# Loads in order of need with a semaphore for each group, the first image in two halves, keys and queries handed over head by head

## The reference

```
xn = group_norm(x)                       # per image
q  = q_w @ xn + q_b                      # 1x1 convolution, 256 -> 256
xd = conv2x2_stride2(xn, ds_w) + ds_b    # 1024 -> 256 pixels
xd = layernorm_over_channels(xd) * ln_w + ln_b
k, v = kv_w @ xd + kv_b                  # two 256 -> 256 products
o  = softmax(q k^T / sqrt(32)) v         # 8 heads of 32 channels
x  = x + proj_w @ o + proj_b
```

## Time and profile before

| | us |
|---|---|
| runs | 898.1, 899.11, 899.64 |
| median | 899.11 |
| profiled execution | 893.1 |
| its span, first to last instruction | 891.3 |
| PE busy | 668.2 (75%) |
| DVE busy | 627.6 (70%) |
| ACT busy | 389.7 (44%) |
| mean granted clock | 0.843 |

### The profile page before, as it was taken

How to read it: one execution, slowest core, us unless ns; L and a number is a source line. 1 busy time by engine, 2 the same in 40 slices (tenths; PEclk the granted TensorE clock), 3 DMA queues, 4 the chain that set the end, 5 groups by cost and what they waited for, 6 DMA issues and landing times.

```text
span 891.3 us, 9082 instructions
## 1 busy us (share of the span) xinstructions
PE 668.2 (75%) x3272; PEld 306.1 (34%) x3272; DVE 627.6 (70%) x1117; ACT 389.7 (44%) x623; POOL 32.8 (4%) x26
## 2 busy tenths in 40 slices
PE   2967984997898999999888879886876766387100
PEld 2622532433232354443334442232343222255100
DVE  2555416614958752776788779987889969986897
ACT  0202451558647467556636267715526453101100
POOL 3200000200001000000020000002000000000000
PEclk9965998899998989899989789998895687685655
DMA  8040024000150000004000000020000100001001
GB/s 303 15 122 2 1 68 116 1 1 1 49 135 2 3 0 1 1 1 118 19 1 1 1 1 1 18 78 1 1 1 0 47 1 1 0 0 48 0 0 47
DMA packets 14990, 26.85 MB, mean 30 GB/s; under 512 B 3250, under 2 KB 6994, under 8 KB 14819
## 3 DMA queue, kind: packets, MB, share of 16 engines
q1 hardware_dynamic: 11648, 22.80, 8.6%
q10 hardware_dynamic: 3298, 3.48, 1.3%
HBM read 14.09 MB, written 4.19 MB: 21 GB/s over the span
## 4 chain that ended last, share of the span: by engine, by line
PE 54%; DVE 24%; ACT 13%; issue 4%; SPq 2%; DMA 2%; DVEq 0%; ACTq 0%
PE aD L1517 5%; PE bA L1409 5%; PE aA L1536 4%; DVE NEGMAX L955 4%; PE bA L1550 4%; PE pp L1442 3%; PE aA L1502 3%; PE bA L1638 3%; PE aD L1482 3%; PE aD L1536 3%; ACT PT L503 2%; PE pp L1409 2%; DVE ACC L1280 2%; DVE PA_ L1271 2%; DVE HB L1266 2%
## 5 line engine op out<-in xcount | busy, mean ns | idle before, releaser
L955 DVE TENSOR_REDUCE NEGMAX<-aD 128x2 f32<-128x512 f32 x128 | 82.8, 685 | 34.2 <-PE aD L1482 32.6
L503 ACT ACTIVATE PT<-aA 128x512 f32<-128x512 f32 x128 | 70.2, 594 | 83.4 <-PE aA L1502 82.7
L1482 PE MATMUL aD<-KST,QST 96*128 96x256 f16 x256 | 54.2, 322 | 28.4 <-DVE NEGMAX L955 16.5
L1280 DVE SCALAR_TENSOR_TENSOR ACC<-PA_,COEF,ACC 128x1024 f32<-128x1024 f32 x48 | 61.5, 1282 | 1.2
L1502 PE MATMUL aA<-QST,KST 98*128 98x512 f16 x128 | 47.7, 426 | 13.7 <-ACT PT L503 9.4
L1271 DVE TENSOR_TENSOR PA_<-HB 128x1024 f32<-128x1024 f32 x40 | 49.0, 1225 | 1.0
L1266 DVE TENSOR_TENSOR HB<-PA_ 128x1024 f32<-128x1024 f32 x40 | 48.7, 1217 | 0.1
L1482 PEld LDWEIGHTS aD<-KST,QST 96*128 96x128 f16 x256 | 20.5, 105 | 78.4 <-DVE NEGMAX L955 40.7
L1517 PE MATMUL aD<-PT,VT 128*32 128x512 f32 x256 | 37.8, 665 | 5.0 <-DVE NEGMAX L955 2.0
L790 POOL TENSOR_TENSOR GA<-GA,PT 128x1024 f32<-128x1024 f32 x8 | 19.3, 2428 | 575.0 <-ACT PT L531 575.0
L972 DVE TENSOR_TENSOR GA<-GA,aD 128x512 f32<-128x512 f32 x16 | 10.9, 684 | 41.5 <-ACT GA L516 33.7
(11 more groups left out here) (298 smaller groups left out, 1325.4 us busy)
## 6 DMA issues: line engine op xcount, KB each, us to landing
XF<-in_x SPq DMA_DIRECT2D x4, 1024.0 KB, 5.1
QST<-QH SPq DMA_DIRECT2D x32, 128.0 KB, 2.4
XR<-in_x SPq DMA_DIRECT2D x4, 1024.0 KB, 5.0
out<-ACC SPq DMA_DIRECT2D x4, 1024.0 KB, 4.0
QST<-QL SPq DMA_DIRECT2D x16, 128.0 KB, 2.5
PS<-in_cw ACTq DMA_DIRECT2D x1, 1152.0 KB
WDS<-in_wds SPq DMA_DIRECT2D x1, 1024.0 KB, 8.2
WP<-in_wp SPq DMA_DIRECT2D x2, 256.0 KB, 10.9
```

Source lines behind the costliest of these rows:

```text
L503: e.activation(PROB[:, 4 * kt + j, :], SLOT[f"aA{j % 2}"][:, :], ACT.Exp)\
L955: e.tensor_reduce(NEGMAX[:, h, 2 * j:2 * j + 2], SLOT[f"aD{j % 2}"][:, :].rearrange("p (t k) -> p t k", t=2), AX.X, ALU.max, negate=True). ...
L1280: e.scalar_tensor_tensor(out=acc, in0=interior(PA_, cc), scalar=COEF[:, cc, k:k + 1], in1=acc, op0=ALU.mult, op1=ALU.add).then_inc(*dve_m. ...
L1482: mm = e.matmul(s[:, t * NK:(t + 1) * NK], QST[0:96, h, qt * P:(qt + 1) * P], KST[0:96, h, :], start=True, stop=True)
```

## The change

The loads on SP keep their order but for WP1 and WP0, which change places, and get four semaphores: `down_loaded` (COL, WDS), `query_loaded` (WQ), `kv_loaded` (WK, WV) and `mid_loaded` (WP1, WP0, XPR, DTP). Each engine waits for those that it uses. x comes as two DMAs, one for each channel half, with a semaphore each, for every image. ACT's 14 loads are issued in its `setup`, behind the group norm's two steps. What needs the middle group (the fold of WP1, WD, the projections) moves behind the keys, into `setup_projections` on PE and DVE.

The front's order becomes: downsampling, queries of block row 0, statistics of the keys' layer norm, queries of block row 1 (second half first), keys, values. The copies on SP are ordered by head at their end, with one semaphore for each `j`; head h < 4 of the scores waits for the five copies of `j` = h and for ACT's one. The order strings of all engines are new. In `SP_ORDER`, the residual load of an image now always stands ahead of the next image's stacking (before, image 2's stood between the queries and the keys of image 3).

```diff
-gn0 ds q0_0 q0_1 q1_0 q1_1 msq0 k vT
+gn0 ds q0_0 q0_1 msq0 q1_1 q1_0 k vT
...
-F5 A3 F5 A3 F5 A2 F2 A1 F2 A2 M1 A1 M3
+F4 A3 F4 A3 F4 A3 F3 A2 M1 A1 M3
...
-            sp.dma_start(XF[:, :, :], x_v[:, 0:CC, :]).then_inc(x_loaded, 16)
+            for cc in range(CC):
+                sp.dma_start(XF[:, cc, :], x_v[:, cc, :]).then_inc(x_loaded[cc], 16)
             sp.dma_start(MAT[:, :, :], mats).then_inc(mats_loaded, 16)
-            for dst, src in ((COL, cols), (WDS, wds), (WQ, wq), (WK, wk), (WV, wv), (WP0, wp0),
-                             (WP1, wp1), (XPR, xpr), (DTP, dtp)):
-                sp.dma_start(dst[tuple(slice(None) for _ in dst.shape)], src).then_inc(early_loaded, 16)
+            for loaded, pairs in ((down_loaded, ((COL, cols), (WDS, wds))), (query_loaded, ((WQ, wq),)),
+                                  (kv_loaded, ((WK, wk), (WV, wv))), (mid_loaded, ((WP1, wp1), (WP0, wp0), (XPR, xpr), (DTP, dtp)))):
+                for dst, src in pairs:
+                    sp.dma_start(dst[tuple(slice(None) for _ in dst.shape)], src).then_inc(loaded, 16)
...
+                def copy(dst, quad, j, src):
+                    sp.dma_start(dst[32 * quad:32 * quad + 32, j:HEADS:4, :], src[32 * j:32 * j + 32, :, :]).then_inc(stacked[j], 16)
+
                 sp.wait_ge(*pe_a.at(b - 1, "st3_1_3"))
...
+                sp.wait_ge(*act_f.at(b, "qh1_0"))
+                for j in range(4):
+                    for quad in (0, 2):
+                        copy(QST, quad, j, QH)
+                yield
+                sp.wait_ge(*dve_f.at(b, "ql1_0"))
+                for j in range(4):
+                    copy(QST, 1, j, QL)
+                yield
+                sp.wait_ge(*act_f.at(b, "kh1"))
+                copy(KST, 0, 0, KH)
+                copy(KST, 0, 1, KH)
+                sp.wait_ge(*dve_f.at(b, "kl1"))
+                copy(KST, 2, 0, KL)
+                copy(KST, 2, 1, KL)
+                for j in (2, 3):
+                    copy(KST, 0, j, KH)
+                    copy(KST, 2, j, KL)
+                yield
...
-                e.wait_ge(early_loaded, 16 * EARLY_N)
+                e.wait_ge(down_loaded, 32)
+                e.wait_ge(kv_loaded, 32)
                 columns("bA0", 0, WK, "kv_ln_b")
-                columns("bA0", 2, WV, "kv_ln_b")
-                columns("bA0", 4, WP1, "ln_b").then_inc(*pe_set.step("fold"))
+                columns("bA0", 2, WV, "kv_ln_b").then_inc(*pe_set.step("fold"))
+
+            def setup_projections():
+
+                e.wait_ge(mid_loaded, 64)
...
-                if h == 0:
-                    e.wait_ge(stacked, 16 * STACK_DMAS * b + 16 * STACK_DMAS)
-                    e.wait_ge(second_stacked, 16 * SECOND_DMAS * b + 16 * SECOND_DMAS)
+                if h < 4:
+                    e.wait_ge(stacked[h], 16 * STACK_DMAS * b + 16 * STACK_DMAS)
+                    e.wait_ge(second_stacked[h], 16 * b + 16)
...
-            def query(b):
-                for m, half in BLOCKS:
+            def query(b, m):
+                for half in (m, 1 - m):
```

More of the change, by code:

```diff
@@ L121 @@
 PE_SETUP = """
-fold wd fold0 wpc
+fold fold1 wd fold0 wpc
 """
@@ L401, in load @@
             def load(b):
-                sp.wait_ge(*pe_f.at(b - 1, "q1_1"))
-                sp.dma_start(XF[:, :, :], x_v[:, b * CC:b * CC + CC, :]).then_inc(x_loaded, 16)
+                sp.wait_ge(*pe_f.at(b - 1, "q1_0"))
+                for cc in range(CC):
+                    sp.dma_start(XF[:, cc, :], x_v[:, b * CC + cc, :]).then_inc(x_loaded[cc], 16)
                 yield
@@ L432, in _ @@
         def _(e):
-            for dst, src in ((S16, small16), (W1S, w1s), (IPX, ipx), (IPZ, ipz), (XB, xb), (XC, xc), (OPW, opw),
-                             (W2Q, w2q), (W2K, w2k), (W2V, w2v), (WP2, wp2), (ROWS, rows), (KIDX, kidx)):
-                e.dma_start(dst[tuple(slice(None) for _ in dst.shape)], src).then_inc(late_loaded, 16)
-            e.dma_start(CW, cw.partition_broadcast(P)).then_inc(late_loaded, 16)
             for s in (act_f, act_a, act_c, act_b, act_d, act_m):
@@ L695, in stream_f @@
                 yield from down(b)
-                yield from query(b)
+                yield from query(b, 0)
                 yield from rstd(b, 0, VAR0, act_f, dve_f)
+                yield from query(b, 1)
                 yield from keys(b)
@@ L741, in setup @@
             def setup():
-                e.wait_ge(early_loaded, 16 * EARLY_N)
+                for dst, src in ((S16, small16), (W1S, w1s), (IPX, ipx), (IPZ, ipz), (XB, xb), (XC, xc), (OPW, opw),
+                                 (W2Q, w2q), (W2K, w2k), (W2V, w2v), (WP2, wp2), (ROWS, rows), (KIDX, kidx)):
+                    e.dma_start(dst[tuple(slice(None) for _ in dst.shape)], src).then_inc(late_loaded, 16)
+                e.dma_start(CW, cw.partition_broadcast(P)).then_inc(late_loaded, 16)
+                e.wait_ge(down_loaded, 32)
                 e.activation(NEGA[:, :], COL[:, :, COLS.index("A_log")], ACT.Exp).then_inc(*act_set.step("expA"))
@@ L835, in group_norm @@
                     for half in range(2):
+                        if l == 0 and half == 0:
+                            e.wait_ge(x_loaded[cc], 16 * b + 16)
                         e.bn_stats(STAT[:, cc, half, :], src(cc, half)).then_inc(*dve.step(f"gn_st{l}_{cc}{half}"))
@@ L1724, in stream_f @@
                     setup()
+                    yield
                 yield from down(b)
-                yield from query(b)
+                yield from query(b, 0)
                 yield from kv_norm(b)
+                yield from query(b, 1)
+                yield from keys(b)
                 if b == 0:
                     setup_projections()
-                yield from keys(b)
+                    yield
             def stream_a(b):
```

128 lines of the change are left out of this document (66 added, 62 removed).

## The result

The changed kernel takes 911.94 us (median of 4 runs, 910.08 to 913.92), the kernel before 899.38 us in the same comparison (4 runs, 898.1 to 901.43): ratio 1.0138, 95% interval 1.0109 to 1.0167. It is **slower** by 1.4%, where the prediction said 889 us. Timed once more beside the last experiments it came to 911.99 us with a ratio of 1.0197 (1.0147 to 1.0246).

A forecast was written before the change was run, and what follows sets the result against it. No single engine bounds it: four images share one interleaved pipeline whose front is paid in full. Part 1 -7.2, Part 2 -2.7, Part 3 0: -9.9 us from 899.11 gives 889 us, range 880 to 898 (own range 886 to 891).

The forecast's parts named there:

- Part 1: Image 0's front: a semaphore per load group lets PE's setup start earlier; downsampling ends at 26.2, not 33.39: -7.2 us.
- the prediction's formula: Downsampling time as 6.97 us plus 0.218 us for each instruction at half clock level; 18.6 such instructions forecast.
- What left the front: ACT's 14 load issues, folding WP1 and WP0, WD and the centring, moved later: hidden behind other work, costing nothing.
- Part 2: Image 0, downsampling to first score: statistics between queries and copies by head, head 0 needing only copies 1 to 15: -2.7 us.
- Part 3: Images 1 to 3 and the new order: up to -4.2 at block 1's group norm against up to +4.5; taken as 0.
- The last sentence of the sum: Behind 57 us: a shift of the front reaches the end whole unless an order holds it back; 889 us.
- Rival C: Image 2's scores start late: up to +13.4 us of products and sums ahead of them, 903 us; chance 0.10.
- A: Image 0's front: the clock rises no earlier, or WV lands late; head gives 7.0 to 7.8, 892 us; chance 0.15.
- B: Images 1 to 3: the new order gives its 4.2 us on top and more at later images, 885 us; chance 0.18.
- D: From 750 us on, DVE must finish image 2's maxima, so the front's gain is used up: 899 us; chance 0.07.
- The residual load ahead of image 3's copies: On SP, image 2's residual load could hold image 3's copies; 7 us of slack, so part of C's chance only.

The follow-up runs named there:

- the old order with the same means: Changed kernel with the order strings of before and statistics again behind both query rows, all else of the change kept: 883.52 us, ratio 0.9844.
- the inner order in image 0: All of the change under the old order strings, plus, in image 0 alone, statistics between the two query rows: 886.22 us, ratio 0.9899 to the kernel before.
- the cut at image 1's front: Changed kernel with its order until image 1's front is through (about 130 us), the old order from there: median 890.99 us, ratio 0.9826 to the kernel before.

## Why the prediction was wrong

- **Part 1 was right in its mechanism**, and gave 1.0 us more than forecast. Fold at 11.58 (forecast 11.72), no DMA in front of it, downsampling at 15.1 (15.16). It took 10.08 us, which by the prediction's formula is 14 instructions at half level (18.6 forecast): the rise came near 21.4, 7.7 us earlier than before and not 5.7. So it ended at 25.2, 8.2 us earlier than before, where 7.2 were forecast. What left the front stayed hidden; the centring of W2V (28.44 to 30.75) is in the chain, as it was before.
- **Part 2 gave 0.5 us and not 2.7.** SP's first copy came at the downsampling's end + 10.8 (9.75 forecast), since the second split query stands behind the centring; the fourteen issues ahead of the last needed copy took 10.2 us and not 9.0. No head after the first waits for its copies, as forecast.
- **Part 3 is the failed step**: "I take 0, between ends of nearly equal size", with +4.5 as the upper end. By the ratios (1.0138 and 1.0197 against 0.9844) the new order costs 3.0 to 3.6%, 26 to 32 us; at like clock 22 us (912.00 against 889.79). The working behind that zero looked at one place, from 140 to 174 us, and there it was fair: against the old order with the same means, image 0's convolution starts 2.0 us earlier (161.88 against 163.84) and PE is 2.2 us behind by 280 us. The three places above where PE then idles lie behind it, and none was in the bounds. That the order was dealt anew on four engines was treated as one trade of a hole against a job, though its strings differ from image 1 to the last.
- **The last sentence of the sum** ("a shift of the front reaches the end whole unless an order holds it back") is borne out in its first half only roughly: with the old order 8.0 us at the head were 14.6 at the end in an execution at 0.851, and 9.9 were 5.4 at 0.837 with the inner order in image 0. The exception decided.
- **Rival C** named the place and part of the size: image 2's first score at 272.15, 6.6 us later than before (forecast 3.5), the total slower. Its price was too low, and its mechanism is not shown. The copies hold that score, issued from 260.55 us on behind the late query, and not the products ahead of it, which leave PE 1.91 us idle; moving the queries ahead gave nothing. A was wrong on the clock, which rose 7.7 us earlier, and B on the order. D's used-up gain is a fact at image 3's last max rows (540.31 against 541.34), but it was used up between 300 and 541 us, partly with DVE full (19.23 of 20 us from 460 on), and not by the window maxima behind 750 that D named.
- **The residual load ahead of image 3's copies** was issued at 407.02 us and those copies began at 418.95: it did not hold them.

What stays open: which of the joined displacements opens the hole at 300 us. The cuts place it, the timeline names the waits; no kernel removed it alone. That the first score came within 1.2 us of the forecast 46.9 is partly luck: part 1 gave 1.0 us more than forecast and part 2 gave 2.2 less.

## What to carry to other kernels

Price a hand-dealt order as a change of its own: compare the means under the old order with the changed kernel before believing a sum that sets the order to zero. A bound taken from one stretch bounds that stretch only; where an order string differs to the end, the unknown is as large as the holes that it can open in every stage. To find where an order loses, cut it: changed up to a landmark, old behind; and do not trust a single product moved by hand, since it takes a bank from the next user.

Compare at like granted clock before reading a step of 1% off a ratio: here the first step of the cuts was mostly the mix of runs.

The best kernel here is the one with all means and the old order, 1.56% faster than before by its ratio and 22 to 32 us faster than the changed one; the cut at image 1's front is about level with it (892.02 against 889.79 us and 878.53 against 878.44).

## What the hardware showed beside it

Two kernels that differ in image 0's front alone reach image 3's first max rows within 0.7 us of each other (482.79 and 483.48) and are 10.7 us apart later (block 2 group norm of image 3 at 748.14 and 758.82). In the first 50 us of this the column of granted clock, the third from the end, differs. All means with the old order, then with image 0's new front:

```profile
480.00:530.00 50.00, 41.05 (x209) 19.89 (x211) 41.88 (x77) 27.38 (x44) 0.00 (x0) 0.90 0.01 1
```

```profile
480.00:530.00 50.00, 42.70 (x189) 20.57 (x187) 38.65 (x70) 24.15 (x39) 0.00 (x0) 0.76 0.00 1
```

At 0.90 PE needed less time for more matmuls (209 against 189) and DVE got 3.2 us more done. The lag is 4.1 us by 530 (the copies of the last max rows are issued at 527.82 and 531.92) and 6.2 by image 3's block 1 group norm (585.16 and 591.36). The last 4.5 us come where the clock of both is alike (0.78 and 0.77 from 600 to 680, 0.78 in both to 760), and stay open. That the clock is the cause and not the trace of another delay is argued from this order of events; no run sets it. The runs of one kernel fall into two groups by this: 877 to 879 us at 0.849 to 0.854 and 888 to 891 us at 0.831 to 0.839 for the kernel with all means. Each run that changes group moves an average of six by some 2 us (an estimate from these numbers), which is why the table of cuts gives the groups apart.
